# Stage 1 of a gated cross-attention and expert layer: ScalarE makes the shift of a tile, VectorE the scales of a group, and the statistics run up to eight tiles ahead

## The chip, the cores and the metric

The kernel runs on one core of a Trainium2 chip. The metric is the device time of one execution in microseconds. A core has five engines with a queue each, which run their own instructions in order and wait for each other by semaphores: TensorE (PE in the profile, PEld its weight loads), VectorE (DVE), ScalarE (ACT), GpSimd (POOL) and SyncE (SP, which here only issues transfers).

## The reference

Four batches of 1024 tokens with 1024 channels, that is 4096 tokens or 32 tiles of 128, pass two gated steps. W and b are the weights of either step, g its gate.

```python
def _L0_xattn_ref(x, adj, W, b):              # x = context (256 wide), adj = layernorm(x)
    si = jnp.einsum('bnd,d->bn', x, Wi[0])
    sj = jnp.einsum('bnd,d->bn', x, Wj[0])
    xij = jax.nn.sigmoid(si[:, :, None] + sj[:, None, :] + b[0])
    return P_ASEM * xij + (1.0 - P_ASEM) * adj

def _L0_ffn_ref(x, wg, W, b):                 # each token goes to the best of 8 experts
    logits = xt @ wg
    probs = jax.nn.softmax(logits, axis=-1)
    idx = jnp.argmax(probs, axis=-1)
    ...
    return out

x = x + jnp.tanh(g_xattn[0]) * _L0_xattn_ref(ctx_512, _layernorm(x), L0_xattn_W, L0_xattn_b)
x = x + jnp.tanh(g_ffn[0]) * _L0_ffn_ref(_layernorm(x), L0_ffn_wg, L0_ffn_W, L0_ffn_b)
```

## The kernel before

**Two stages.** Stage 1 makes the first step for every token, finds each token's expert and its place in that expert's list, and writes the row to a table in DRAM, sorted by expert. Stage 2 goes through the table in slots of 128 rows, loads each expert's weights, multiplies (L1151) and scatters the results. The change touches stage 1 alone. The sigmoid is written as a half tanh, and the first step becomes, for a token, x * a + b + c * tanh(...), where a (the scale) comes from the variance of x, and b (the shift) from the mean of x times a and the mean of the tanh.

**Tiles, groups, slots.** Stage 1 runs over 32 tiles `t`; four make a group `g`, and `r` is a tile's place in it (`GR = 4`). A tile lies in `xr`, in one of 16 slots (`RX = 16`, slot `t % 16`). SP loads the first 16 tiles at once. Tile `t` from 16 on is loaded (`next_tile`, L304) after the store of tile `t - 16` has landed (`row_stored`).

**The order.** Each engine's order is written out by hand, as a loop over the tiles. For one tile:

- VectorE: `stats` (two BN statistics, L797) and `moments` (L802) of tile `t + LEAD`, with `LEAD = 6`; `add_tanh(t)` (L808) adds the tanh. For a group: `choose` (L818 to L824, picks the expert; in the loop at `r == 1` of the next group) and `position` (L830 to L837, the places in the table; at `r == 2` of the next group).
- ScalarE: `half_tanh` (L633) of tile `t + 3`, which also sums the tanh; there are four tanh buffers, so it waits for `add_tanh` four tiles before it. `copy_turned(t)` (L641), and per group `logits_copy` (L648). The context's `context_copy`, `context_sums` and `context_spread` stand between, once per group up to tile 17.
- POOL: `norm_scalars(g)` (L470 to L475) makes the row numbers, the root of the variance and the scales of a group; `linear(t)` is the shift (L480, one element per token) and x * a + b (L482, 1024 elements). POOL makes the tile two ahead, and stores (`store`, L490, an indirect transfer) tiles of the group before: at `r == 3` the first two, behind `linear(t + 2)`; the other two at the next `r == 0` and `r == 1`. A store waits for `position` of its group.
- TensorE: `turn_tile(t)` (L1075), `logits_by_token` (L1097, at `r == 1` for the group before), `rank` (at `r == 2`), `route(t - 1)` (L1087), and the context's matmuls.

Semaphores tie them: `mv_ready` counts moments, `th_ready` tanh, `lin_ready` linears, `xc_ready` finished tiles, `pos_ready` positions of groups, `x_landed` loads of a slot. VectorE's own loop before the change is

```python
for t in range(T):
    add_tanh(t)
    if r == 2 and g > 0:
        position(g - 1)
    if t + LEAD < T:
        stats(t + LEAD)
        moments(t + LEAD)
    if r == 1 and g > 0:
        choose(g - 1)
```

## Time and profile before

| | us |
|---|---|
| three runs: median (lowest to highest) | 615.59 (614.61 to 615.63) |
| the profiled execution | 615.98 |
| its span, first to last instruction | 614.3 |

| engine | busy us | share of the span | instructions |
|---|---|---|---|
| TensorE | 506.9 | 83% | 2889 |
| VectorE | 404.8 | 66% | 529 |
| POOL | 361.5 | 59% | 537 |
| ScalarE | 293.0 | 48% | 426 |

The shares are means over both stages. Stage 1 is the stretch up to about 157 us, in which TensorE is 55 to 77% busy; from 200 us on it is nearly always busy. The rows below are of five views: windows (busy time of each engine in a stretch), the chain of waits (followed back from the last instruction, at each step to what released it), timelines of one engine in order of time, groups of instructions by line, and transfers from issue to landing. Times of rows are us from the start of the span; in brackets stands how long the engine was idle ahead of the instruction, and who ended that.

### The profile page before, as it was taken

The page shows a single profiled execution, that of the slowest core. Times are in us where ns is not written, and L with a number is a line of the kernel's source. Part 1 is how long each engine was busy: PE and PEld are TensorE (multiplying, and loading weights), DVE is VectorE, ACT ScalarE, POOL GpSimd, SP SyncE. Part 2 cuts the span into 40 slices and gives each one's busy share as a digit, 9 for nine tenths or more (in the row PEclk, how much of TensorE's full clock was granted, in tenths as well). Part 3 has the DMA queues.
Part 4 walks back from the last instruction along what each step waited for, and adds up shares of the span by engine and source line. Part 5 has one row for each costly group of instructions (what it writes and reads, how often), then busy time and mean ns, then how long its engine had stood idle before and what let it go on. Part 6 is the DMA issues. An engine that isn't in the chain of part 4 may idle for free.

```text
span 614.3 us, 14917 instructions
## 1 busy us (share of the span) xinstructions
PE 506.9 (83%) x2889; PEld 416.4 (68%) x2890; DVE 404.8 (66%) x529; ACT 293.0 (48%) x426; POOL 361.5 (59%) x537
## 2 busy tenths in 40 slices
PE   4676676666404999999999999999999999989980
PEld 4565565545303887887888888788888888878860
DVE  1777557785786777777777577778657857764230
ACT  2486556754312455455544454555445534553330
POOL 2596878889611364565555645655556465556662
PEclk9598778887755999999999999999999999999995
DMA  6952776783788588787888688897759777885520
GB/s 229 359 203 95 251 246 237 220 308 131 268 275 225 165 253 218 240 261 227 244 250 238 191 224 240 241 252 238 233 150 273 219 224 200 238 235 164 192 100 8
DMA packets 87751, 134.63 MB, mean 219 GB/s; under 512 B 11696, under 2 KB 69552, under 8 KB 87728
## 3 DMA queue, kind: packets, MB, share of 16 engines
q1 hardware_dynamic: 72464, 80.28, 46.6%
q0 software_dynamic: 15264, 54.06, 24.9%
q8 instruction: 12, 0.20, 0.1%
q14 instruction: 11, 0.09, 0.0%
HBM read 100.49 MB, written 35.91 MB: 222 GB/s over the span
## 4 chain that ended last, share of the span: by engine, by line
PE 21%; issue 19%; POOL 17%; DVE 16%; ACT 12%; ACTq 7%; DMA 2%; POOLq 2%; DVEq 1%; SPq 1%
PE pair L1151 13%; DVE xt L876 5%; DVE pair L884 5%; ACT rb L699 4%; ACT xt L691 4%; POOL scal L525 3%; POOL scal L528 3%; POOL table L490 2%; PE pair L1075 2%; PE pair L1066 2%; ACTq L732 2%; DVE xr L808 2%; DMA gates<-in_L_xattn_b 1%; ACT th L633 1%; POOL out_x L569 1%
## 5 line engine op out<-in xcount | busy, mean ns | idle before, releaser
L1151 PE MATMUL pair<-wt,xt 128*128 x1728 | 398.9, 393 | 31.8 <-DVE xt L876 27.3
L1151 PEld LDWEIGHTS pair<-wt,xt 128*128 128x128 f32 x1728 | 326.1, 189 | 104.3 <-issue 33.6
L536 POOL TENSOR_TENSOR rows<-rows,rb 128x1024 f32<-128x1024 f32 x37 | 89.5, 2420 | 2.9 <-ACT rb L713 1.6
L876 DVE TENSOR_TENSOR xt<-pair,xt 128x1024 f32 (+1 forms) x38 | 46.5, 1224 | 66.0 <-ACT xt L691 66.0
L685 ACT ACTIVATE wt<-pair 128x1024 f32 x56 | 57.6, 1028 | 55.9 <-DVE pair L884 51.7
L713 ACT ACTIVATE rb<-bias_bc,scal 128x1024 f32 (+1 forms) x37 | 46.0, 1244 | 71.1 <-POOL scal L532 71.1
L891 DVE TENSOR_TENSOR wt<-pair,wt 128x1024 f32 x56 | 67.9, 1212 | 13.0 <-ACT wt L685 13.0
L884 DVE STREAM_TRANSPOSE pair<-w_raw 128x1024 f32<-128x1024 f32 x56 | 69.4, 1239 | 1.0
L1075 PE MATMUL pair<-ident,xr 128*128 128x128 f32 x256 | 43.3, 324 | 31.6 <-DVE xr L808 31.5
L1075 PEld LDWEIGHTS pair<-ident,xr 128*128 128x128 f32 x256 | 35.9, 171 | 38.1 <-DVE xr L808 32.3
L295 POOL DMA_DIRECT2D rows<-table x38 | 23.2, 610 | 57.6 <-issue 27.0
L871 DVE STREAM_TRANSPOSE pair<-xb 128x1024 f32<-128x1024 f32 x38 | 47.8, 1259 | 12.9 <-issue 6.4
L569 POOL DMA_INDIRECT out_x<-rows,scatter_row x36 | 39.6, 1100 | 27.8 <-issue 27.8
L903 DVE SCALAR_TENSOR_TENSOR rows<-pair,scal,rows 128x1024 f32 x36 | 46.2, 1284 | 8.4 <-PE pair L1151 4.2
L490 POOL DMA_INDIRECT table<-xr,pos x32 | 42.9, 1341 | 10.3 <-issue 6.8
L641 ACT ACTIVATE xc_tr<-pair 128x1024 f32<-128x1024 f32 x32 | 32.8, 1025 | 32.7 <-PE pair L1075 32.5
L691 ACT ACTIVATE xt<-pair 128x1024 f32 (+1 forms) x38 | 39.0, 1027 | 16.3 <-DVE pair L871 10.6
L699 ACT ACTIVATE rb<-rows 128x1024 f32 (+1 forms) x37 | 38.9, 1052 | 14.4 <-POOL rows L536 14.4
L808 DVE SCALAR_TENSOR_TENSOR xr<-th,c,xr 128x1024 f32<-128x1024 f32 x32 | 41.8, 1305 | 5.3 <-POOL xr L482 5.2
L482 POOL TENSOR_SCALAR xr<-xr,ln_a,ln_b 128x1024 f32<-128x1024 f32 x32 | 41.2, 1289 | 3.2
L797 DVE BATCH_NORM_STATS2 raw<-xr 128x6 f32<-128x512 f32 x64 | 40.7, 677 | 3.2 <-DMA xr<-in_x 3.2
L705 ACT ACTIVATE ez<-rows,scal 128x8 f32 (+1 forms) x37 | 11.1, 301 | 61.1 <-POOL scal L525 61.1
(138 smaller groups left out, 407.5 us busy)
## 6 DMA issues: line engine op xcount, KB each, us to landing
w_raw<-in_L_ffn_W SPq DMA_DIRECT2D x264, 128.0 KB, 3.0
xb<-table SPq DMA_DIRECT2D x156, 128.0 KB
rows<-table POOLq DMA_DIRECT2D x38, 520.0 KB, 5.0
xr<-in_x SPq DMA_DIRECT2D x32, 512.0 KB, 6.3
ctx_in<-in_ctx SPq DMA_DIRECT2D x8, 512.0 KB, 5.3
bias_bc<-in_L_ffn_b SPq DMA_DIRECT2D x8, 512.0 KB, 6.2
out_x<-rows,scatter_row POOLq DMA_INDIRECT x36, 3.7
table<-xr,pos POOLq DMA_INDIRECT x32, 5.7
```

What stands on the lines that cost most here:

```text
L490: nc.gpsimd.indirect_dma_start(out=table, out_offset=bass.IndirectOffsetOnAxis(ap=pos[:, t:t + 1], axis=0), in_=xr[:, s, :], in_offset=Non ...
L536: nc.gpsimd.tensor_tensor(rows[:, k, 0:H], rows[:, k, 0:H], rb[:, :], ALU.add).then_inc(base_ready, 1)
L685: nc.scalar.activation(wt[:, bass.ds(par, 1), 0, :, bass.ds(column + P * n, P)].rearrange("p a k o -> p (a k) o"), ps[:, :].rearrange("p ( ...
L691: nc.scalar.activation(xt[:, bass.ds(k, 1), 0, :, :].rearrange("p a k n -> p (a k n)"), ps[:, :], ACT.Copy).then_inc(xt_hi_ready, 1)
L699: nc.scalar.activation(rb[:, :], rows[:, at, 0:H].rearrange("p a h -> p (a h)"), ACT.Square, accum_out=scal[:, at, 0:1].rearrange("p a e - ...
L808: nc.vector.scalar_tensor_tensor(out=xr[:, s, 0:H], in0=th[:, t % RTH, :], scalar=c2[:, 0:1], in1=xr[:, s, 0:H], op0=ALU.mult, op1=ALU.add ...
L871: nc.vector.transpose(turned(ps), blocked(xb[:, k, :, :])).then_inc(xb_turned, 1)
L876: nc.vector.tensor_tensor(xt[:, at, 1, :, :].rearrange("p a k n -> p (a k n)"), ps[:, :], xt[:, at, 0, :, :].rearrange("p a k n -> p (a k ...
L884: nc.vector.transpose(turned(ps), blocked(w_raw[:, n, :, :])).then_inc(w_turned, 1)
L891: nc.vector.tensor_tensor(where[:, :, 1].rearrange("p a k o -> p (a k) o"), ps[:, :].rearrange("p (k o) -> p k o", k=K), where[:, :, 0].re ...
L1075: last = nc.tensor.transpose(xt_ps[t % 2][:, P * k:P * (k + 1)], xr[:, slot_of(t), P * k:P * (k + 1)], ident[:, :])
L1151: last = nc.tensor.matmul(out_ps[r % 2][:, HALF * h:HALF * (h + 1)], xt[:, r % RING, x_part, k, :], wt[:, bass.ds(par, 1), w_part, k, HALF ...
```

## The change

Of `norm_scalars`, POOL keeps the row numbers, the addition of epsilon and the root; this is now `row_numbers(g)`, called at `r == 0` in place of `r == 2`. The scales `ln_a` and their product with the mean, `ln_ma` (now with the other sign), are made by VectorE in a new `norm_scalars(g)`, after `add_tanh` at `r == 1`. The shift `ln_b` is made by ScalarE in a new `shift(t)`, one tile behind the tanh and ahead of `copy_turned`. `linear` on POOL is one instruction and waits for `scales_of_tile` and `shift_ready`. VectorE's statistics start with six tiles as before, and then at each tile up to two more are made, as long as they are at most eight ahead (`t + LEAD + 2`). Three semaphores are new.

```diff
-                link(nc.gpsimd.tensor_scalar(ln_a[:, four], ln_r[:, four], c_ln[:, 0:1], 1.0, ALU.mult, ALU.add))
-                link(nc.gpsimd.tensor_tensor(ln_ma[:, four], of_group(g, MEAN), ln_a[:, four], ALU.mult))
+                nc.gpsimd.tensor_tensor(ln_r[:, four], ln_v[:, four], minus_half[:, :],
+                                        ALU.pow).then_inc(root_ready, 1)
             def linear(t):
                 s = slot_of(t)
-                pool.wait_ge(th_ready, t + 1)
-                link(nc.gpsimd.tensor_scalar(ln_b[:, t:t + 1], xr[:, s, TH:TH + 1], nc2h[:, 0:1], ln_ma[:, t:t + 1],
-                                             ALU.mult, ALU.subtract))
+                pool.wait_ge(scales_of_tile, t // GR + 1)
+                pool.wait_ge(shift_ready, t + 1)
...
-            norm_scalars(0)
+            row_numbers(0)
             linear(0)
             linear(1)
             for t in range(T):
                 g, r = t // GR, t % GR
-                if r == 2 and g + 1 < NG:
-                    norm_scalars(g + 1)
+                if r == 0 and g + 1 < NG:
+                    row_numbers(g + 1)
...
+            def shift(t):
+                act.wait_ge(th_ready, t + 1)
+                act.wait_ge(scales_of_tile, t // GR + 1)
+                nc.scalar.activation(ln_b[:, t:t + 1], xr[:, slot_of(t), TH:TH + 1], ACT.Identity,
+                                     scale=nc2h[:, 0:1], bias=ln_ma[:, t:t + 1]).then_inc(shift_ready, 1)
...
             for t in range(RTH - 1):
                 half_tanh(t)
+                if t:
+                    shift(t - 1)
             for t in range(T):
                 g, r = t // GR, t % GR
                 if t + RTH - 1 < T:
                     half_tanh(t + RTH - 1)
                 if r == 1 and g > 0:
                     logits_copy(g - 1)
+                if t + RTH - 2 < T:
+                    shift(t + RTH - 2)
                 copy_turned(t)
...
+            def norm_scalars(g):
+                four = slice(GR * g, GR * (g + 1))
+                dve.wait_ge(root_ready, g + 1)
+                link(nc.vector.tensor_scalar(ln_a[:, four], ln_r[:, four], c_ln[:, 0:1], 1.0, ALU.mult, ALU.add))
+                nc.vector.scalar_tensor_tensor(out=ln_ma[:, four], in0=of_group(g, MEAN), scalar=-1.0,
+                                               in1=ln_a[:, four], op0=ALU.mult, op1=ALU.mult).then_inc(scales_of_tile, 1)
...
             for t in range(LEAD):
                 stats(t)
                 moments(t)
+                if t == GR:
+                    norm_scalars(0)
+            seen = LEAD
             for t in range(T):
                 g, r = t // GR, t % GR
                 add_tanh(t)
+                if r == 1 and g + 1 < NG:
+                    norm_scalars(g + 1)
                 if r == 2 and g > 0:
                     position(g - 1)
-                if t + LEAD < T:
-                    stats(t + LEAD)
-                    moments(t + LEAD)
+                for n in range(2):
+                    if seen < T and seen <= t + LEAD + 2:
+                        stats(seen)
+                        moments(seen)
+                        seen += 1
```

VectorE around tiles 8 and 9, before: add_tanh(8), the statistics of tile 14 (which wait for the load of slot 14), add_tanh(9), the statistics of tile 15, and the first row of choose(1).

```order
L808 SCALAR_TENSOR_TENSOR xr<-th,c2,xr 128x1024 [waits lin_ready]
L797 BN_STATS raw<-xr 128x6 [waits x_landed14]
L797 BN_STATS raw<-xr 128x6
L802 BN_AGGR xr<-raw 128x2 [waits raw_ready]
L808 SCALAR_TENSOR_TENSOR xr<-th,c2,xr 128x1024 [waits lin_ready]
L797 BN_STATS raw<-xr 128x6 [waits x_landed15]
L797 BN_STATS raw<-xr 128x6
L802 BN_AGGR xr<-raw 128x2 [waits raw_ready]
L818 TENSOR_REDUCE top<-pair3 128x4 [waits by_token]
```

The same place now, from add_tanh(8) to choose(1); L826 is add_tanh, L808 the statistics, L819 and L820 the scales of group 3, L836 begins choose.

```order
L826 SCALAR_TENSOR_TENSOR xr<-th,c2,xr 128x1024 [waits lin_ready]
L808 BN_STATS raw<-xr 128x6 [waits x_landed0]
L808 BN_STATS raw<-xr 128x6
L813 BN_AGGR xr<-raw 128x2 [waits raw_ready]
L826 SCALAR_TENSOR_TENSOR xr<-th,c2,xr 128x1024 [waits lin_ready]
L819 TENSOR_SCALAR ln_a<-ln_r,c_ln 128x4 [waits root_ready]
L820 SCALAR_TENSOR_TENSOR ln_ma<-xr,ln_a 128x4 [waits dve_step]
L808 BN_STATS raw<-xr 128x6 [waits x_landed1]
L808 BN_STATS raw<-xr 128x6
L813 BN_AGGR xr<-raw 128x2 [waits raw_ready]
L836 TENSOR_REDUCE top<-pair3 128x4 [waits by_token]
```

The statistics behind add_tanh(8) are now those of tile 16, the second tile of slot 0, and behind add_tanh(9) those of tile 17, the second of slot 1.

ScalarE around tiles 6 and 7, before: half_tanh(9), copy_turned(6), half_tanh(10), copy_turned(7), half_tanh(11).

```order
L633 ACTIVATE th,xr<-sj,si_half 128x1024 [waits mv_ready,xc_ready,si_ready,sj_ready]
L641 ACTIVATE xc_tr<-pair0 128x1024 [waits routed,xc_turned]
L633 ACTIVATE th,xr<-sj,si_half 128x1024 [waits mv_ready,xc_ready,si_ready,sj_ready]
L641 ACTIVATE xc_tr<-pair1 128x1024 [waits routed,xc_turned]
L633 ACTIVATE th,xr<-sj,si_half 128x1024 [waits mv_ready,xc_ready,si_ready,sj_ready]
```

The same place now; L640 is the shift, here of tiles 8 and 9, and L647 is copy_turned.

```order
L633 ACTIVATE th,xr<-sj,si_half 128x1024 [waits mv_ready,xc_ready,si_ready,sj_ready]
L640 ACTIVATE ln_b<-xr,ln_ma,nc2h 128x1 [waits scales_of_tile,th_ready]
L647 ACTIVATE xc_tr<-pair0 128x1024 [waits routed,xc_turned]
L633 ACTIVATE th,xr<-sj,si_half 128x1024 [waits mv_ready,xc_ready,si_ready,sj_ready]
L640 ACTIVATE ln_b<-xr,ln_ma,nc2h 128x1 [waits scales_of_tile,th_ready]
L647 ACTIVATE xc_tr<-pair1 128x1024 [waits routed,xc_turned]
```

What `linear(9)` on POOL waits for now, shift(9), stands behind copy_turned(6) and half_tanh(10); before it waited for half_tanh(9), ahead of both.

## Rows read from the trace of the kernel before

**Rows 1.** Windows: busy us (instructions) of PE, PEld, DVE, ACT, POOL; granted clock; DMA.

```profile
140.00:160.00 20.00, 14.74 (x172) 11.68 (x173) 10.76 (x19) 8.89 (x11) 17.80 (x16) 0.75 0.28 113
...
300.00:614.00 314.00, 293.54 (x1281) 240.24 (x1279) 198.16 (x188) 142.75 (x206) 175.87 (x278) 0.98 0.71 207
```

**Rows 2.** Chain of waits, 110 to 157 us, shares by line.

```profile
by line: POOL table L490 32.2%; issue 28.9%; POOL ln_b L480 11.8%; POOL xr L482 11.6%; POOL ln_r L473 4.6%; POOL ln_v L472 3.4%; DVE xr L808 2.8%; ACT th L633 2.7%; POOL ln_a L474 1.2%; POOLq L489 1.1%; POOL ln_ma L475 0.9%; POOL xr L470 0.
```

**Rows 3.** Timeline of VectorE: start us, us, line, operation, [idle before].

```profile
53.41 0.19 DVE L837 TENSOR_REDUCE pos<-place 128x4 uint32<-128x32 f32 x1
...
58.84 1.28 DVE L797 BATCH_NORM_STATS2 raw<-xr 128x6 f32<-128x512 f32 x2
...
60.27 1.23 DVE L808 SCALAR_TENSOR_TENSOR xr<-th,c,xr 128x1024 f32<-128x1024 f32 x1
...
67.68 0.19 DVE L818 TENSOR_REDUCE top<-pair 128x4 f32<-128x32 f32 x1 [4.73 <-PE pair L1097]
...
73.05 0.19 DVE L837 TENSOR_REDUCE pos<-place 128x4 uint32<-128x32 f32 x1
```

**Rows 4.** Timeline of POOL: the stores of tiles 0 and 12.

```profile
55.45 2.01 POOL L490 DMA_INDIRECT table<-xr,pos  x1 [0.19 <-issue]
...
112.71 1.10 POOL L490 DMA_INDIRECT table<-xr,pos  x1 [0.17 <-issue]
```

**Rows 5.** Timeline of SP: the loads of tiles 16 and 28 are issued.

```profile
59.87 0.34 SPq L304 DMA_DIRECT2D xr<-in_x  x1
...
116.22 0.33 SPq L304 DMA_DIRECT2D xr<-in_x  x1
```

**Rows 6.** DMA: the same two loads alone, size and us from issue to landing.

```profile
xr<-in_x SPq DMA_DIRECT2D x1, 512.0 KB, 4.2
...
xr<-in_x SPq DMA_DIRECT2D x1, 512.0 KB, 3.6
```

**Rows 7.** Timeline of TensorE: logits by token (L1097), turns of a tile (L1075).

```profile
66.58 1.06 PE L1097 MATMUL pair<-fold,bias_bc 128*128 128x8 f32 x8 [1.43 <-ACT bias_bc L648]
...
71.59 1.07 PE L1075 MATMUL pair<-ident,xr 128*128 128x128 f32 x8
...
84.44 1.32 PE L1097 MATMUL pair<-fold,bias_bc 128*128 128x8 f32 x8 [1.70 <-ACT bias_bc L648]
...
90.27 1.86 PE L1075 MATMUL pair<-ident,xr 128*128 128x128 f32 x8
...
103.88 1.06 PE L1097 MATMUL pair<-fold,bias_bc 128*128 128x8 f32 x8 [1.85 <-ACT bias_bc L648]
```

**Rows 8.** Timeline of VectorE, later: ends of position, add_tanh(21) and add_tanh(31).

```profile
92.51 0.19 DVE L837 TENSOR_REDUCE pos<-place 128x4 uint32<-128x32 f32 x1
...
111.16 0.19 DVE L837 TENSOR_REDUCE pos<-place 128x4 uint32<-128x32 f32 x1
...
117.92 1.23 DVE L808 SCALAR_TENSOR_TENSOR xr<-th,c,xr 128x1024 f32<-128x1024 f32 x1
...
156.20 1.28 DVE L808 SCALAR_TENSOR_TENSOR xr<-th,c,xr 128x1024 f32<-128x1024 f32 x1
```

**Rows 9.** Timeline of ScalarE: copy_turned(10) and half_tanh(14).

```profile
73.45 1.02 ACT L641 ACTIVATE xc_tr<-pair 128x1024 f32<-128x1024 f32 x1
74.35 1.15 ACT L633 ACTIVATE th<-sj,si_half 128x1024 f32<-128x1024 f32 x1
```

**Rows 10.** Groups by line, 40:170; two of the page: busy us, mean ns | idle.

```profile
L480 POOL TENSOR_SCALAR ln_b<-xr,nc2h,ln_ma 128x1 f32<-128x1 f32 x26 | 12.7, 488 | 10.2 <-ACT th L633 9.0
...
L474 POOL TENSOR_SCALAR ln_a<-ln_r,c_ln 128x4 f32<-128x4 f32 x6 | 3.6, 594 | 0.6
...
L475 POOL TENSOR_TENSOR ln_ma<-xr,ln_a 128x4 f32<-128x4 f32 x6 | 2.2, 372 | 0.5
...
L705 ACT ACTIVATE ez<-rows,scal 128x8 f32 (+1 forms) x37 | 11.1, 301 | 61.1 <-POOL scal L525 61.1
...
L797 DVE BATCH_NORM_STATS2 raw<-xr 128x6 f32<-128x512 f32 x64 | 40.7, 677 | 3.2 <-DMA xr<-in_x 3.2
```

More of the change, by code:

```diff
@@ L214, in build @@
         lin_ready = sem("lin_ready")
+        root_ready = sem("root_ready")
+        scales_of_tile = sem("scales_of_tile")
+        shift_ready = sem("shift_ready")
         xc_ready = sem("xc_ready")
@@ L270, in slot_of, with of_group @@
             return t % RX
+        def of_group(g, col):
+            s = slot_of(GR * g)
+            return xr[:, s:s + GR, col:col + 1].rearrange("p r a -> p (r a)")
         def tile_of(rows_of, t):
@@ L460, in _, with row_numbers @@
             nc.gpsimd.tensor_copy(cum[:, 0, :], cum0_f[:, :]).then_inc(cum_ready, 1)
-            pool.wait_ge(scales_ready, 1)
-            def of_group(g, col):
-                s = slot_of(GR * g)
-                return xr[:, s:s + GR, col:col + 1].rearrange("p r a -> p (r a)")
-            def norm_scalars(g):
+            def row_numbers(g):
                 four = slice(GR * g, GR * (g + 1))
@@ L655, in _ @@
                 context_spread(g)
+            act.wait_ge(scales_ready, 1)
             for t in range(RTH - 1):
                 half_tanh(t)
+                if t:
+                    shift(t - 1)
             for t in range(T):
```

1 line of the change is left out of this document (removed).

## Prediction

> **What bounds the kernel now.** I read the windows first, then the chain of waits, then VectorE's, POOL's, TensorE's and ScalarE's timelines of stage 1, and last how long single transfers took to land. The profiled execution took 615.98 us, its span is 614.3; the median of the three runs is 615.59, 0.39 below it. The change touches stage 1 alone, which ends when VectorE has finished add_tanh(31), 1.28 us after 156.20 [rows 8]. From 300 us on TensorE is busy 293.5 of 314 us [rows 1]; that stage starts later or earlier with the end of stage 1 and is otherwise as before, so I forecast how far add_tanh(31) moves and carry this to the end one to one.
>
> Stage 1 has two halves. Between 110 and 157 us the chain of waits runs nearly all through POOL: the stores L490 32%, "issue" (between POOL's own instructions) 29%, the shift L480 12%, the linear L482 12% [rows 2], and POOL is busy 17.8 of 20 us there [rows 1]. This is what the change relieves. Before that no engine is full; the work goes round VectorE, TensorE, ScalarE and POOL once per group of four tiles. add_tanh(9) starts at 60.27 [rows 3], add_tanh(21) at 117.92 [rows 8]: three groups in 57.65 us, 19.2 us each.
>
> **Where tile 16 comes from.** There are 16 tile slots. Tile 16 is loaded when tile 0 has been stored, and tile 0 is stored when position(0) has told where. position(0) ends at 53.60 (53.41 + 0.19) [rows 3]; store(0) starts at 55.45 [rows 4]; its landing lets SP issue the load at 59.87 [rows 5], which takes 4.2 us [rows 6], so tile 16 is there at 64.07. VectorE asks for it right behind position(1), at 73.24 (73.05 + 0.19) [rows 3], two tiles after the place that this change gives to the same statistics: 9 us of slack. In the changed order (shown with the change) stats(16) stands right behind add_tanh(8), where stats(14) started at 58.84 [rows 3]. That is 5.2 us before tile 16 lands. **VectorE would stand there, and behind it in its queue stand add_tanh(9), the scales, choose(1), add_tanh(10) and position(1)**, and so the next store, and so the load of tile 20. The same place comes back at tiles 12, 16 and 20, which ask for tiles 20, 24 and 28. A loop closes that was open: position, store, load, stats, position. From position(0) to stats(16) VectorE has only two statistics (1.43 each, 58.84 to 60.27) and two add_tanh (1.23) [rows 3], 5.3 us, against a store and a load that took 8.6 us the first time (55.45 to 59.87, and 4.2) and 7.1 the last (112.71 to 116.22, and 3.6) [rows 4 to 6], with 7.8 and 7.9 between. No ordering inside 5.3 us hides 7.1.
>
> The Trainium skill (DMA: Bandwidth & Descriptors, Anatomy of one DMA) gives for a transfer of POOL's kind about 2.0 us plus bytes over 436 GB/s. For half a megabyte that makes 3.2 us, and I estimate from this page 6.4 us for a store and a load together; the rows say 7.1 to 8.6. With the page's price the four waits would each be some 1.5 us shorter, which would take about 6 us off the sum below; the measurement decides.
>
> **The change part by part.**
>
> *Start, up to add_tanh(9): later by 8.8 us.* Three things. (1) Two more tiles' statistics come before add_tanh(2), 2 x 1.43 [rows 3], and each shift on ScalarE is one small instruction; the nearest row with a scale from memory is ez, 0.30 us [rows 10], and nine of them stand ahead of linear(9), 2.7 us. The two delays lie side by side and some of either falls into idle time: I take 2 us, bounds 0 and 3. (2) linear(9) used to wait for half_tanh(9). Now it waits for shift(9), which stands behind copy_turned(6) and half_tanh(10): 74.35 - 73.45 = 0.9 for the copy, 1.15 for the tanh [rows 9], 0.3 for the shift: 2.3 us. Store(0) stands behind linear(9) on POOL. Bounds 0 (position(0) is later still) and 2.8. (3) Tile 16 is then there at 55.45 + 2 + 2.3 + 7.9 (the mean of the four) = 67.6, its statistics take 1.43, and add_tanh(9) starts at 69.1 instead of 60.27. Least: 55.45 + 7.1 + 1.4 = 63.95, later by 3.7. Most: 55.45 + 5.8 + 8.6 + 1.4 = 71.25, later by 11.0.
>
> *Three groups, add_tanh(9) to add_tanh(21): 23.6 us each for 19.2, later by 13.1 us.* From one landing to the next:
> A, landing to the start of logits_by_token: statistics 1.43, add_tanh 1.23 [rows 3], 0.1 between, and TensorE's turn of the tile, 1.07 us in one row, 1.86 in another [rows 7]: 3.8 to 4.6; I take 4.3, nearer the slower turn, since TensorE stands idle ahead of it.
> B, logits to the end of position: 66.58 to 73.24, 84.44 to 92.70 (92.51 + 0.19), 103.88 to 111.35 (111.16 + 0.19) [rows 3, 7, 8], that is 6.7, 8.3 and 7.5; I take the mean, 7.5. In it lie choose, add_tanh, and on TensorE the context of the next batch and the second turn; none of this changes.
> C, position to the next store: 1.85 before (53.60 to 55.45), 1.4 in the last of these groups (111.35 to 112.71) [rows 3, 4, 8]. The store stands behind linear(t+5), and that behind the same copy, tanh and shift as above, 2.3 us more. The four places took 1.85, 2.25, 1.5 and 1.4 before; the mean of the last three, 1.7, and 2.3 make 4.0, of which I take 3.9; bounds 1.4 (no detour) and 4.5.
> D, store to landing: 7.9; bounds 7.1 and 8.6.
> Sum 23.6, bounds 19.0 and 26.0. Three times 4.4 is 13.1; bounds -0.6 and +20.4.
> POOL and ScalarE use the stall: everything up to linear(t+3) and the other two stores of the group is done when the tile lands. That is why I charge the wait once per group and not per tile.
>
> *Tail, add_tanh(21) to add_tanh(31): shorter by 5 us.* It took 156.20 - 117.92 = 38.3 us [rows 8]. POOL loses ten shifts, 0.49 each [rows 10] and 0.1 between: 5.9 us; and of two groups the scale and its product, 0.59 + 0.37 [rows 10], 1.9 us. At most 7.8, if POOL holds the whole stretch. But after the last wait it stands idle until ScalarE has copied tile 21 and made shift(24), and row_numbers(7) waits for stats(31); so two thirds of it, 5, bounds 0 and 7.8.
>
> *At nothing:* the scales on VectorE (two instructions of 128x4 per group) stand right behind add_tanh, where VectorE next waits for a tile or for the logits; without that cover they cost under 1 us per group, and the root they wait for is made during the stall. SP's later tile loads push the first weight loads later, but they are wanted only after add_tanh(31), which moves more. The steps behind stage 1 keep their order.
>
> **Sum.** 8.8 + 13.1 - 5.0 = +16.9. 615.98 + 16.9 = 632.9 on the profile's scale, 632.5 as a median.
>
> **The rivals.**
> *POOL is what counts, and the kernel gets faster.* Place: POOL, 110 to 157 us. If tiles landed before VectorE asks, only the relief is left: -7.8 in the tail, some 608 us. For it: the chain [rows 2]. It decides where store and load together take under 5.3 us after position; no row comes near, and the slots can't be freed sooner. Chance 0.07.
> *The loop closes, but at its shortest.* Groups of 19.0 us, as now, because the waits that VectorE has today for the logits (it is idle 4.73 us ahead of 67.68 [rows 3]) are eaten by the stall. Then 8.8 - 0.6 - 5 = +3.2: 619 us. For it: part of what VectorE waits for today is indeed done during the stall; against it: TensorE's context work in B lies behind the logits, not ahead of them. Chance 0.15. With the least start as well (3.7) and the whole tail relief it would be about -4.7, 611; I leave 0.02 for that and 0.04 for a sum within 0.2%.
> *The loop at its longest.* TensorE's granted clock is 0.75 of full speed on the mean in 140 to 160 us [rows 1], so it changes between its two levels (1.2 and 2.4 GHz). If it stays at the lower because TensorE idles more, every turn takes 1.86 for 1.07 [rows 7], and B is 8.3: 26.0 us a group, 8.8 + 20.4 - 5 = +24, 640 us. Chance 0.12.
> *The change does not do what it says.* From tile 16 on the statistics can't run eight ahead, since the slots hold 16 tiles of which the last eight are not stored yet. That is the forecast itself, not a rival.
>
> **How the numbers follow.** The forecast has 0.60, the longest loop 0.12, the shortest 0.15, sums within 0.2% (1.2 us, about what a measurement of this kernel can tell from no change) 0.04, faster 0.09. The range runs from the shortest loop, 619, to 643, a little over the longest; 0.13 of the chances lie below it and some hundredths above. Faster 0.09, same 0.04, slower 0.87.
>
> **What would show it.** Right: VectorE's BN statistics show idle time put down to the loading of xr, at four places, each after the add_tanh of tiles 8, 12, 16 and 20, some 5 to 7 us each and about 20 to 30 in all (before: 3.2 in the whole run [rows 10]); add_tanh(9) near 69, add_tanh(21) near 140, add_tanh(31) near 173; add_tanh(9), (13), (17), (21) 22 to 25 us apart; stage 2 as long as before. POOL's chain between 110 and 157 is gone. Wrong: statistics that never wait, or waits that only replace those for the logits, so that add_tanh(21) stands near 120; then the start and the groups were charged for time that was idle already. If the groups are 19 but the start is 9 later, step B or C was counted twice.

## The result, and the profile after

The changed kernel took 645.35 us (median of 3 runs, 643.31 to 645.74) for 615.59: 1.0464 times as long, interval 1.0427 to 1.0501. That is 29.8 us slower where 16.9 was forecast; the direction was right, and the time lies above the range (619 to 643). The profiled execution has a span of 643.7 us for 614.3, 29.4 more.

In the changed code the statistics are L808 and L813, the scales L819 and L820, add_tanh L826, choose L836 to L842, position L848 to L855 (VectorE); the root L475, the linear L482, the store L490 (POOL); the shift L640 (ScalarE); the turn of a tile L1100 and the logits by token L1122 (TensorE).

First VectorE's waits in 20 to 190 us (what was waited for: us in total, times, longest us), which answer to the last line of [rows 10], 3.2 us in the whole run before:

```profile
DVE raw L808 <- DMA xr<-in_x: 24.6, 6, 5.6
DVE place L853 <- PE pair L1135: 18.4, 7, 3.9
DVE top L836 <- PE pair L1122: 14.1, 7, 3.7
```

The same in VectorE's timeline, beside [rows 3] and [rows 8] (in brackets the idle time before and what ended it): the statistics of tiles 16, 20, 24 and 28 wait for their loads; add_tanh(9) follows the first and add_tanh(21) the last of them; add_tanh(31) ends the stage. The two rows of L855 are the ends of position(0) and position(1).

```profile
60.06 0.19 DVE L855 TENSOR_REDUCE pos<-place 128x4 uint32<-128x32 f32 x1
...
70.97 1.28 DVE L808 BATCH_NORM_STATS2 raw<-xr 128x6 f32<-128x512 f32 x2 [5.55 <-DMA xr<-in_x]
...
72.42 1.23 DVE L826 SCALAR_TENSOR_TENSOR xr<-th,c,xr 128x1024 f32<-128x1024 f32 x1
...
84.03 0.19 DVE L855 TENSOR_REDUCE pos<-place 128x4 uint32<-128x32 f32 x1
...
94.90 1.29 DVE L808 BATCH_NORM_STATS2 raw<-xr 128x6 f32<-128x512 f32 x2 [5.51 <-DMA xr<-in_x]
...
118.82 1.28 DVE L808 BATCH_NORM_STATS2 raw<-xr 128x6 f32<-128x512 f32 x2 [5.50 <-DMA xr<-in_x]
...
142.55 1.28 DVE L808 BATCH_NORM_STATS2 raw<-xr 128x6 f32<-128x512 f32 x2 [5.31 <-DMA xr<-in_x]
...
143.99 1.23 DVE L826 SCALAR_TENSOR_TENSOR xr<-th,c,xr 128x1024 f32<-128x1024 f32 x1
...
184.79 1.27 DVE L826 SCALAR_TENSOR_TENSOR xr<-th,c,xr 128x1024 f32<-128x1024 f32 x1
```

The start, in the timelines of POOL and VectorE: POOL waits for VectorE's moments before it makes the root of group 1, and VectorE waits for that root before it makes the scales.

```profile
30.75 0.14 POOL L472 IOTA xr<- 128x4 int32 x1 [1.84 <-DVE xr L813]
...
33.08 0.23 DVE L819 TENSOR_SCALAR ln_a<-ln_r,c_ln 128x4 f32<-128x4 f32 x1 [1.26 <-POOL ln_r L475]
```

POOL's timeline: linear(5) and linear(8), which wait for ScalarE's shift, and the stores of tiles 0 and 4 [rows 4].

```profile
45.08 1.20 POOL L482 TENSOR_SCALAR xr<-xr,ln_a,ln_b 128x1024 f32<-128x1024 f32 x1 [5.10 <-ACT ln_b L640]
...
60.12 1.20 POOL L482 TENSOR_SCALAR xr<-xr,ln_a,ln_b 128x1024 f32<-128x1024 f32 x1 [5.14 <-ACT ln_b L640]
...
64.09 1.25 POOL L490 DMA_INDIRECT table<-xr,pos  x1 [0.20 <-issue]
...
88.03 1.01 POOL L490 DMA_INDIRECT table<-xr,pos  x1 [0.16 <-issue]
```

POOL's linears in the page's groups (busy us, mean ns | idle before):

```profile
L482 POOL TENSOR_SCALAR xr<-xr,ln_a,ln_b 128x1024 f32<-128x1024 f32 x32 | 44.5, 1390 | 70.4 <-ACT ln_b L640 70.3
```

The chain of waits from 144 to 186 us, the tail, where before it ran through POOL [rows 2]:

```profile
by line: PE pair L1100 37.7%; DVE xr L826 22.8%; PE pair L1122 9.1%; PE pair L1112 6.2%; DVE raw L808 5.7%; DVE pick L838 5.6%; issue 2.1%; DVE xr L813 1.5%; DVE top L836 1.4%; DVE place L853 1.4%; DVE pick L837 1.4%; DVE top_pick L840 1.4%
```

POOL is gone from it, as foreseen, but the tail did not get shorter. Taken from the starts of add_tanh(9), (21) and (31), the 29.4 us are:

| | before, us | after, us | more | forecast |
|---|---|---|---|---|
| start: to add_tanh(9) | 60.27 | 72.42 | +12.15 | +8.8 |
| three groups: to add_tanh(21) | 57.65 | 71.57 | +13.9 | +13.1 |
| tail: to add_tanh(31) | 38.28 | 40.80 | +2.5 | -5.0 |
| from add_tanh(31) to the end | 458.1 | 459.0 | +0.9 | 0 |

The groups came as forecast; the tail is off by 7.5 us and the start by 3.4.

### The profile page after: what moved, and what is told of

Same layout as the page of the kernel before. It is cut to its first block, busy times and chain, and to the rows that moved or that the text cites. A ratio compares the mean times of both kernels' runs of the same rounds, so it can differ in the third digit from the quotient of the medians.

```text
span 643.7 us, 14973 instructions
## 1 busy us (share of the span) xinstructions
PE 532.7 (83%) x2889; PEld 437.1 (68%) x2890; DVE 411.8 (64%) x545; ACT 302.1 (47%) x458; POOL 330.1 (51%) x489
## 4 chain that ended last, share of the span: by engine, by line
PE 24%; issue 17%; DVE 17%; POOL 11%; ACT 11%; DMA 8%; ACTq 6%; SPq 2%; POOLq 2%; DVEq 1%
PE pair L1176 15%; PE pair L1100 4%; DVE xt L901 4%; DVE pair L909 4%; ACT rb L710 3%; DMA xr<-in_x 3%; ACT xt L702 3%; POOL scal L525 3%; POOL scal L528 2%; DVE xr L826 2%; DMA table<-xr,pos 2%; DVE raw L808 2%; DMA out_x<-rows,scatter_row 2%; ACT th L633 2%; PE pair L1091 1%
## 5 line engine op out<-in xcount | busy, mean ns | idle before, releaser
L1100 PE MATMUL pair<-ident,xr 128*128 128x128 f32 x256 | 56.7, 395 | 43.9 <-DVE xr L826 43.9
L696 ACT ACTIVATE wt<-pair 128x1024 f32 x56 | 57.6, 1028 | 55.9 <-DVE pair L909 51.9
L1100 PEld LDWEIGHTS pair<-ident,xr 128*128 128x128 f32 x256 | 46.2, 209 | 52.7 <-DVE xr L826 45.4
L482 POOL TENSOR_SCALAR xr<-xr,ln_a,ln_b 128x1024 f32<-128x1024 f32 x32 | 44.5, 1390 | 70.4 <-ACT ln_b L640 70.3
L808 DVE BATCH_NORM_STATS2 raw<-xr 128x6 f32<-128x512 f32 x64 | 40.7, 677 | 25.2 <-DMA xr<-in_x 25.2
L647 ACT ACTIVATE xc_tr<-pair 128x1024 f32<-128x1024 f32 x32 | 32.7, 1021 | 49.3 <-PE pair L1100 49.3
L710 ACT ACTIVATE rb<-rows 128x1024 f32 (+1 forms) x37 | 38.9, 1052 | 14.1 <-POOL rows L536 14.1
L490 POOL DMA_INDIRECT table<-xr,pos x32 | 34.7, 1083 | 16.8 <-DVE pos L855 10.1
L826 DVE SCALAR_TENSOR_TENSOR xr<-th,c,xr 128x1024 f32<-128x1024 f32 x32 | 40.2, 1260 | 3.7 <-POOL xr L482 3.7
```

The lines of the kernel that those rows point to most:

```text
L696: nc.scalar.activation(wt[:, bass.ds(par, 1), 0, :, bass.ds(column + P * n, P)].rearrange("p a k o -> p (a k) o"), ps[:, :].rearrange("p ( ...
L710: nc.scalar.activation(rb[:, :], rows[:, at, 0:H].rearrange("p a h -> p (a h)"), ACT.Square, accum_out=scal[:, at, 0:1].rearrange("p a e - ...
L808: last = nc.vector.bn_stats(raw[:, t % 2, h, :], xr[:, s, HALF * h:HALF * (h + 1)])
L826: nc.vector.scalar_tensor_tensor(out=xr[:, s, 0:H], in0=th[:, t % RTH, :], scalar=c2[:, 0:1], in1=xr[:, s, 0:H], op0=ALU.mult, op1=ALU.add ...
L1100: last = nc.tensor.transpose(xt_ps[t % 2][:, P * k:P * (k + 1)], xr[:, slot_of(t), P * k:P * (k + 1)], ident[:, :])
```

## Experiments

Times are medians; each ratio is to the kernel before on the same chip, with its 95% interval. The parts of stage 1 are read from add_tanh's starts as above, position(0) from its end. The "stretch" of VectorE in the tail is worked out from the trace: for each of its instructions there, the duration above that of an undisturbed one of the same kind, summed. half_tanh(0), which no edit reaches, starts between 20.3 and 22.5 us in these kernels (22.3 before, 22.5 after), so a microsecond or two between two starts can be scatter. From there on the edits count: from half_tanh(0) to linear(0) it is 1.92 us before the change and 2.84 after it, because shift(0) now stands behind half_tanh(1). Each part is read from one trace of its kernel.

| kernel | median, us | ratio | add_tanh(9) | three groups | tail | stretch |
|---|---|---|---|---|---|---|
| before | 615.59 | 1 | 60.3 | 57.6 | 38.3 | 1.9 |
| after | 645.35 | 1.0464 | 72.4 | 71.6 | 40.8 | 4.4 |
| e1 six ahead | 624.01 | 1.0118 [1.0056, 1.0180] | 68.0 | 56.7 | 41.0 | 4.0 |
| e2 eight ahead alone | 628.12 | 1.0192 [1.0131, 1.0253] | 64.1 | 65.6 | 39.4 | 2.7 |
| e3 shift at once | 637.46 | 1.0352 [1.0283, 1.0421] | 69.4 | 65.4 | 41.4 | 4.1 |
| e4 twenty slots | 624.91 | 1.0145 [1.0087, 1.0202] | 65.4 | 56.2 | 41.9 | 6.9 |
| f1 after, extra turns | 648.93 | 1.0553 [1.0526, 1.0581] | 71.3 | 74.2 | 40.4 | 4.7 |
| f2 before, extra turns | 613.24 | 0.9949 [0.9923, 0.9975] | 62.8 | 50.7 | 38.8 | 2.6 |
| f3 twenty slots, at once | 624.29 | 1.0149 [1.0123, 1.0175] | 63.9 | 55.9 | 42.7 | 7.2 |
| f4 f3 with extra turns | 621.01 | 1.0097 [1.0072, 1.0123] | 63.8 | 51.5 | 42.6 | 8.3 |
| g1 twenty slots, neither move | 616.72 | 1.0026 [0.9997, 1.0055] | 61.3 | 56.4 | 38.3 | 1.9 |
| g2 g1 with the scales on VectorE | 618.10 | 1.0042 [1.0025, 1.0060] | 63.8 | 56.2 | 38.4 | 2.5 |
| h2 g1 with the shift on ScalarE | 624.67 | 1.0144 [1.0102, 1.0186] | 62.1 | 57.8 | 45.0 | 8.0 |
| g4 linear on ScalarE | 641.56 | 1.0416 [1.0366, 1.0465] | 75.5 | 61.6 | 45.6 | 0.4 |
| h1 f3, small instruction back | 620.07 | 1.0085 [1.0057, 1.0114] | 62.8 | 57.0 | 38.7 | 2.3 |
| i1 after, small instruction back | 646.70 | 1.0491 [1.0433, 1.0548] | 73.3 | 76.3 | 39.5 | 1.1 |
| h3 before, extra turns from tile 9 | 611.90 | 0.9924 [0.9898, 0.9950] | 60.1 | 52.0 | 37.1 | 1.9 |

### The loop: e1, e2 and e4

**e1** is the changed kernel with the statistics six ahead again; the shift and the scales stay on the engines where the change puts them, the scales of a group stand behind choose, where its statistics are there, and POOL makes the root one tile later, behind the linear.

```diff
-                if r == 0 and g + 1 < NG:
-                    row_numbers(g + 1)
...
+                if r == 1 and g + 1 < NG:
+                    row_numbers(g + 1)
...
-                for n in range(2):
-                    if seen < T and seen <= t + LEAD + 2:
-                        stats(seen)
...
+                if t + LEAD < T:
+                    stats(t + LEAD)
+                    moments(t + LEAD)
                 if r == 1 and g > 0:
                     choose(g - 1)
+                if r == 1 and g + 1 < NG:
+                    norm_scalars(g + 1)
```

> The change without its run-ahead: statistics six tiles ahead as before, shift on ScalarE and scales on VectorE as in the change. Theory L (the loop store, load, statistics, position sets the time): VectorE no longer waits for loads, the groups from add_tanh(9) to add_tanh(21) go back from 23.9 to 19 to 20 us, and what is left is the shift's place on ScalarE: 614 to 624 us. Rival S (the shift stands too late on ScalarE, and the waits for loads only sit where VectorE would wait for linear anyway): groups stay near 23 us, 638 us or more. Rival C (TensorE's lower clock is the cause, whatever the wait): 630 to 640.

**e2** is the kernel before with only the run-ahead of the change (the lines that e1 takes out, put into it).

> The kernel before with the statistics up to eight tiles ahead and nothing else; POOL keeps shift and scales. L: the loop closes as in the change, but the store no longer waits for a copy, a tanh and the shift (2.3 us), so groups of 21 to 22 us, four waits for loads of about 4 us: 626 to 634 us. S: 613 to 618 us, as the kernel before.

**e4** is the changed kernel with more room: tile 16 no longer waits for tile 0 to be stored.

```diff
-    RX = 16
+    RX = 20
```

(th, ctx_in and xc_tr move into memory that is used only after stage 1, and the counts of stores per slot follow.)

> The change with 20 tile slots in place of 16 (tanh, context and turned tiles lie where the even weights lie later, to make the room). Tile 20 takes the slot of tile 0, and VectorE asks for it four tiles later than it asks for tile 16 in the change. L: no waits for loads, groups 19 to 20 us, 614 to 624 us as in the run with six ahead. S: waits move to linear, 635 us or more. C: between, with the clock of TensorE still at 0.6 in stage 1.

e1 and e4 take the loop apart at two different places, and both take 20 to 21 us off; e1 came to the upper end of what was expected, e4 to 0.9 us above it. The groups are back at 56 to 57 us, and the statistics wait for loads no longer than before. The group of e4, and below it that of e2, from their pages:

```profile
L808 DVE BATCH_NORM_STATS2 raw<-xr 128x6 f32<-128x512 f32 x64 | 40.7, 677 | 3.4 <-DMA xr<-in_x 3.4
...
L797 DVE BATCH_NORM_STATS2 raw<-xr 128x6 f32<-128x512 f32 x64 | 40.7, 677 | 24.3 <-DMA xr<-in_x 24.3
```

e2, which has the run-ahead and nothing else, waits 24.3 us for loads and loses 8 us in the groups. So the loop is shown, from both sides. What e1 and e4 leave, 8 to 9 us, is neither run-ahead nor slots: it is in the start and the tail. (The start of e1 has a price of its own: VectorE waits 3.95 us there for the root that comes later, so that its 68.0 can't be laid beside the others.)

### The place of the shift: e3 and f3

**e3** puts the shift right behind its own tanh on ScalarE instead of one tile later.

```diff
-                if t:
-                    shift(t - 1)
+                shift(t)
...
-                if t + RTH - 2 < T:
-                    shift(t + RTH - 2)
+                if t + RTH - 1 < T:
+                    shift(t + RTH - 1)
                 copy_turned(t)
```

> The change with each shift right behind its own tanh on ScalarE, one place earlier. L: four waits for loads remain, each group 2 us shorter (the store comes earlier), and the start and the tail lose a copy and a tanh ahead of linear: 626 to 636 us. S: the waits go with the detour, 612 to 620 us.

**f3** is e3 with the 20 slots of e4.

> 20 slots and the shift right behind its own tanh together: neither the loop over the loads nor the detour is left, POOL is relieved. If these two hold all that the change loses: 605 to 614 us, the tail 31 to 35. K: the tail stays near 40, now on TensorE and VectorE: 614 to 622 us.

With 16 slots the late place costs 3 us of the start and 2 us in each group: the store stands behind the linear, the linear behind the shift, and all of it is inside the loop. With 20 slots it costs 1.5 us of the start, and the median does not move (624.91 and 624.29). In neither is the tail better: 41.4 and 42.7. Both miss what was expected: e3 by 1.5 us, and f3 lies above either of its two cases, in the tail too.

### TensorE's clock: f1, f2 and f4

The granted clock in 80 to 140 us is lower after than before; the columns are busy us (instructions) of PE, PEld, DVE, ACT and POOL, then the granted clock and DMA. After:

```profile
80.00:100.00 20.00, 14.09 (x107) 11.78 (x106) 10.47 (x19) 11.09 (x20) 11.09 (x11) 0.59 0.47 161
100.00:120.00 20.00, 15.15 (x133) 12.27 (x132) 9.35 (x22) 11.10 (x20) 8.32 (x9) 0.58 0.54 175
```

To see what that costs, TensorE turns the identity eight more times ahead of each tile from tile 2 on, in the time in which it would wait for add_tanh. **f1** is the changed kernel, **f2** the kernel before and **f4** f3 with this edit:

```diff
-                pe.wait_ge(xc_ready, t + 1)
                 if t >= 2:
                     pe.wait_ge(xc_copied, t - 1)
+                    for n in range(8):
+                        nc.tensor.transpose(xt_ps[t % 2][:, P * (n % K):P * (n % K + 1)], ident[:, :], ident[:, :])
+                pe.wait_ge(xc_ready, t + 1)
```

> The change, with eight more turns of the identity on TensorE ahead of each turn of a tile, while it waits for add_tanh; the real turn overwrites them. They cost 1.1 us a tile at the higher clock, 2.0 at the lower, mostly in idle time. Theory K (what the relief of POOL uncovers is the loop of choose, add_tanh, turn, rank, position, and that loop is long because TensorE runs at the lower clock): turns fall from 1.97 to near 1.1 us, groups from 23.9 to 21.5 to 22.5, the tail from 40.8 to 36 to 38: 631 to 638 us. Rival (the tail is long because linear waits for a shift that stands behind copy_turned): 643 to 649 us, the tail stays at 40 to 41 or grows by the added turns.

> The kernel before with the same eight added turns. K: its tail is POOL's, so that stays at 38; the groups lose up to 1 us each: 608 to 615 us. If the added turns delay TensorE where it doesn't wait: 616 to 622.

> The same with the eight added turns. K: tail 35 to 37, groups 17 to 18.5 us, 603 to 612 us, faster than the kernel before. Rival: as the run without them, or some us longer.

The groups of the turns of a tile in 20 to 190 us, before, after and in f1 (busy us, mean ns | idle before), and f1's wait for loads:

```profile
L1075 PE MATMUL pair<-ident,xr 128*128 128x128 f32 x256 | 43.3, 324 | 31.6 <-DVE xr L808 31.5
...
L1100 PE MATMUL pair<-ident,xr 128*128 128x128 f32 x256 | 56.7, 395 | 43.9 <-DVE xr L826 43.9
...
L1102 PE MATMUL pair<-ident,xr 128*128 128x128 f32 x256 | 40.1, 308 | 41.6 <-DVE xr L826 41.5
...
DVE raw L808 <- DMA xr<-in_x: 29.6, 8, 6.7
```

In f1 the turns of a tile fall from 395 to 308 ns a matmul, and yet the groups take 74.2 us and VectorE still waits 29.6 us for loads. It is not the clock that closes the loop. How much of the loop's length the clock makes f1 can't tell, since its own extra turns lie in the loop. Theory K, that the low clock is what the relief of POOL uncovers, expected 631 to 638 us of f1 and 603 to 612 of f4; they took 648.93 and 621.01. Where the loop is out of the way, the clock counts in the groups, and by more than expected: f4's fall from f3's 55.9 to 51.5 us, and f2's fall from 57.6 to 50.7 us, at a granted clock of 1.00, the 2.4 GHz level all the time, for 0.79 in the same 40 us before. f2:

```profile
80.00:100.00 20.00, 16.75 (x203) 14.62 (x199) 14.40 (x30) 13.56 (x20) 17.19 (x21) 1.00 0.75 248
100.00:120.00 20.00, 16.22 (x203) 13.73 (x204) 14.60 (x35) 12.85 (x22) 17.31 (x21) 1.00 0.71 249
```

The tail gains nothing by it: in f2 it is POOL's (the chain there runs through L490 and ln_b), in f1 and f4 the extra turns stand on the chain themselves, with 13.9% and 8.3% of it, since tiles follow each other closely there.

### The two moves apart: g1, g2, h2 (and g3)

All have 20 slots and the statistics eight ahead, so that the loop is out of the way. **g1** has neither move, **g2** only the scales on VectorE, **h2** only the shift on ScalarE, at once; f3 has both. In g2 and h2 POOL makes the root as early as in the change (`r == 0`), and in h2 it has one more instruction of 128x4 per group, which negates the scales' product.

> The kernel before with 20 tile slots and the statistics eight ahead; shift and scales stay on POOL. It is the ground on which the two moves are told apart. Loop theory (all that eight ahead costs is the wait for a slot): no wait for xr above 3.5 us, groups 18.7 to 19.2 us each, tail 38 to 39, 615 to 617 us. Rival (the two more statistics ahead of add_tanh(2) cost their 2.9 us of start whatever the slots): add_tanh(9) at 63 or later, 618 to 620 us.

> 20 slots, eight ahead, the scales of a group on VectorE as in the change, the shift on POOL as before. The changed kernel with 20 slots and the shift at once took 624.3 us. If the scales are what costs the start (VectorE waits for POOL's root ahead of stats and choose, and POOL's linear waits for VectorE): add_tanh(9) at 63 to 64, position(0) ending near 57, 620 to 623 us. If the shift on ScalarE is what costs: as with neither move, 616 us, add_tanh(9) at 61.

> g3_shift_alone with the linear as before (multiply, add), since there the linear that multiplies and subtracts took 3.78 us on POOL for 1.20 and hid everything else; POOL negates the scales in one more 128x4 instruction per group. With neither move it took 616.7 us with a tail of 38.3, with the scales alone 618.1 and 38.4. If the shift makes the tail longer, by bursts of linears against VectorE: tail 41 to 43, 620 to 624 us. If it takes both moves together: tail 38 to 39, 616 to 618 us; there POOL's scales still part its linears.

The first form of h2, **g3**, kept the sign of the scales and let the linear subtract:

```diff
-                                        ALU.mult, ALU.add).then_inc(lin_ready, 1)
+                                        ALU.mult, ALU.subtract).then_inc(lin_ready, 1)
```

> 20 slots, eight ahead, the shift on ScalarE right behind its tanh, the scales on POOL as before (its linear subtracts). If the shift is what costs, through ScalarE's queue or because POOL's linears then run in bursts against VectorE: tail 41 to 43 us, 620 to 623 us, and VectorE's instructions beside POOL's are stretched by 4 us or more in the tail (1.9 before). If the scales are what costs: tail 37 to 38, 614 to 616 us.

It took 673.55 us (1.0943, 1.0883 to 1.1003) and says nothing on the shift, since the linear that subtracts takes three times as long on POOL (g3's timeline of POOL; 1.20 us elsewhere):

```profile
105.10 3.79 POOL L484 TENSOR_SCALAR xr<-xr,ln_a,ln_b 128x1024 f32<-128x1024 f32 x1
109.06 2.12 POOL L492 DMA_INDIRECT table<-xr,pos  x1 [0.18 <-issue]
111.24 3.78 POOL L484 TENSOR_SCALAR xr<-xr,ln_a,ln_b 128x1024 f32<-128x1024 f32 x1
```

The other three give an answer. With slots enough, eight ahead alone is within the noise of before (1.0026). The scales, with the earlier root, cost 2.5 us of the start; in all, the noise can't tell g2 from g1 (1.0042 and 1.0026, intervals overlap). The shift costs 1.2%, most of it in the tail: 45.0 us for 38.3, more than the 41 to 43 expected. Of g2 I had thought it possible that the scales were the culprit, at 620 to 623 us; the start came as that case says, the median did not.

g2 shows one thing more. POOL's instructions that start in its tail take 30.1 us for 33.7 in g1's, and the tail is the same, 38.4 for 38.3. The chain of waits of g2 in 120 to 160 us says why:

```profile
by line: PE pair L1092 31.9%; DVE xr L818 19.5%; PE pair L1104 9.2%; PE pair L1114 7.8%; ACT th L636 5.3%; issue 4.7%; DVE pick L830 3.4%; DVE raw L800 3.0%; DVE onehot L834 2.6%; ACT bias_bc L651 2.5%; DVE pick L829 1.5%; DVE top L828 1.5%
```

No POOL: TensorE's turns, add_tanh and choose make a second path that is just as long as POOL's was. In g2 it also carries the scales, so that how long it was in the kernel before is not measured; it can't have been over 38.3 us. POOL's relief, with the scales handed to VectorE, was worth nothing here.

### Why the tail grows: g4, h1 and i1

As long as the linear is on POOL, VectorE's stretch in the tail mostly goes with its length: 1.9 to 2.5 us where the tail is 38.3 to 38.4, 6.9 to 8.3 where it is 42 to 45. In f3's tail the onehot of choose, 0.18 us elsewhere, takes 2.67 us, and ends where two linears end that POOL ran without a break. VectorE's timeline:

```profile
143.46 0.19 DVE L840 TENSOR_TENSOR xr<-pair,top 128x32 f32<-128x32 f32 x1
143.57 2.67 DVE L841 TENSOR_TENSOR onehot<-pick,top_pick 128x32 bf16<-128x32 f32 x1
146.16 1.27 DVE L825 SCALAR_TENSOR_TENSOR xr<-th,c,xr 128x1024 f32<-128x1024 f32 x1
```

POOL's timeline of the same 3 us:

```profile
143.84 2.36 POOL L482 TENSOR_SCALAR xr<-xr,ln_a,ln_b 128x1024 f32<-128x1024 f32 x2
```

The stretched onehot is on f3's chain of waits, with 12.4% of 120 to 164 us:

```profile
by line: PE pair L1099 33.2%; DVE xr L825 21.2%; DVE onehot L841 12.4%; PE pair L1121 6.7%; PE pair L1111 5.9%; issue 5.4%; DVE raw L807 2.7%; ACT th L633 1.4%; DVE top L835 1.4%; DVE pick L836 1.4%; DVE place L852 1.4%; DVE pick L837 1.4%;
```

Before, a small instruction (ln_b) with a wait behind it stood between any two linears. **g4** takes the linear off POOL:

```diff
+                act.wait_ge(shift_ready, t + 1)
+                nc.scalar.activation(xr[:, s, 0:H], xr[:, s, 0:H], ACT.Identity,
+                                     scale=ln_a[:, t:t + 1], bias=ln_b[:, t:t + 1]).then_inc(lin_ready, 1)
```

> 20 slots, eight ahead, scales on VectorE, shift at once, and the linear of a tile on ScalarE too, right behind copy_turned of three tiles earlier, so that POOL keeps only the root, the row numbers and the stores. With the linear on POOL it took 624.3 us with a tail of 42.7, in which VectorE's instructions were stretched by 7.2 us. Theory of collisions (VectorE and POOL hold each other up, and a relieved POOL runs its linears back to back against add_tanh and choose): the stretch falls under 2 us in the tail, the tail to 36 to 38, 617 to 620 us. Rival (TensorE and VectorE's own steps set the tail, the stretch lies beside other waits): tail 41 to 43, 623 to 626 us. Third: ScalarE, 1.15 us more per tile, becomes the bound: groups of 20 us or more, 627 us or above.

The stretch falls to 0.4 us, but ScalarE, busy 48.6 of 60 us in 80 to 140, becomes the bound (its third case), so g4 decides nothing on the tail. **h1** does it the other way round: f3, with POOL's small instruction given back; its result is written to a spare column and not used.

```diff
+                link(nc.gpsimd.tensor_scalar(spare[:, t:t + 1], xr[:, s, TH:TH + 1], nc2h[:, 0:1], ln_ma[:, t:t + 1],
+                                             ALU.mult, ALU.add))
                 nc.gpsimd.tensor_scalar(xr[:, s, 0:H], xr[:, s, 0:H], ln_a[:, t:t + 1], ln_b[:, t:t + 1],
```

> The changed kernel with 20 slots and the shift at once (624.3 us, tail 42.7), to which POOL gets back its small 128x1 instruction ahead of each linear; its result goes to a spare column and is not used. POOL has more work, nobody has less. Theory of bursts (a relieved POOL runs linear behind linear, and VectorE's instruction that falls beside the pair waits for both: the onehot of 143.57 took 2.67 us for 0.18): the small instruction with its wait parts the linears, the tail falls to 38 to 40, 619 to 621 us. Rival (ScalarE's part of the shift sets the tail, or TensorE and VectorE alone): tail 42 to 44, 624 to 627 us.

POOL does more, nobody does less, and the kernel is faster: the tail falls from 42.7 to 38.7 us, the stretch from 7.2 to 2.3, and the ratios of h1 and f3 have intervals that do not touch. The same place in h1, VectorE's timeline:

```profile
141.19 0.18 DVE L844 TENSOR_TENSOR onehot<-pick,top_pick 128x32 bf16<-128x32 f32 x1
141.29 1.43 DVE L828 SCALAR_TENSOR_TENSOR xr<-th,c,xr 128x1024 f32<-128x1024 f32 x1
```

And POOL's:

```profile
141.99 0.94 POOL L483 TENSOR_SCALAR spare<-xr,nc2h,ln_ma 128x1 f32<-128x1 f32 x1
143.03 1.20 POOL L485 TENSOR_SCALAR xr<-xr,ln_a,ln_b 128x1024 f32<-128x1024 f32 x1
144.20 0.34 POOL L483 TENSOR_SCALAR spare<-xr,nc2h,ln_ma 128x1 f32<-128x1 f32 x1
```

Here it is POOL's small instruction that waits (0.94 for 0.34) while add_tanh runs. **i1** makes h1's edit on the changed kernel itself.

> The changed kernel itself (16 slots, shift late), with POOL's small 128x1 instruction back ahead of each linear, its result unused. If the bursts hold in the changed kernel as in the one with 20 slots (where this took the tail from 42.7 to 38.7): tail 38 to 39.5 for 40.8, start and groups as they are, 643 to 644 us. If the tail there is long because the last load's stall leaves POOL and VectorE out of step, and not for bursts: tail 40 to 42, 645 to 647 us. Either way the waits for xr stay at 24 to 26 us in all.

Its tail is 39.5 us for 40.8 and the stretch 1.1 for 4.4, but the kernel is no faster: with 16 slots the small instruction lies ahead of the store and so inside the loop. From position to store i1 takes 4.7, 6.3, 4.5 and 6.3 us for 3.8, VectorE waits 34.0 us for loads, where 24 to 26 were expected, and the groups grow by 4.7 us. Most of i1's tail has POOL on its chain again. So of the changed kernel's tail the bursts are worth about 1.3 us, by one trace of each, less than with 20 slots.

### A faster kernel: h3

**h3** is the kernel before with f2's extra turns from tile 9 on only (`range(8 if t > 8 else 0)`).

> The kernel before with eight more turns of the identity on TensorE ahead of each tile's turn from tile 9 on (from tile 2 on it took 613.24, groups of 16.9 us for 19.2, but add_tanh(9) at 62.8 for 60.3). If those of tiles 2 to 8 only delayed the start: add_tanh(9) at 60 to 61, groups of 17 us, 610 to 612 us. If the start needs them to get TensorE to its higher clock: 613 to 615 us.

611.90 us, 0.9924 (0.9898 to 0.9950): the start is back at 60.1, the groups keep most of the gain (52.0). It is faster than both kernels, if by less than 1%; TensorE does work that nobody needs, to keep its clock (1.00 in 80 to 120 us).

## Why the prediction was right and wrong

**The loop: right.** Statistics that stand 5.2 us before their tile, four waits of 5.3 to 5.6 us, nothing else in VectorE's queue able to pass: as forecast, and e1, e2 and e4 show it. The group of 23.9 us (forecast 23.6) splits from the rows above. A, landing at 70.97 to logits by token at 75.47 (TensorE's timeline, not shown): 4.5 for 4.3. B, to the end of position(1) at 84.22: 8.75 for 7.5. C, to the store at 88.03: 3.8 for 3.9. D, to the next landing at 94.90: 6.9 for 7.9. B lies above the bound that I gave it (8.3) and D below its own (7.1); that the sum fits is luck. In B lie turns of TensorE at a lower clock (395 ns a matmul for 324); that these made it longer is argued and not shown, since f1 has the higher clock and no shorter group, but also the extra turns. D came out at 6.7 to 6.9 us at all four places. Here the Trainium skill (DMA: Bandwidth & Descriptors, Anatomy of one DMA), from which I had estimated 6.4, was nearer than my mean of the rows of before. Those loads stood beside more other traffic (DMA share 0.70 to 0.89 in 80 to 140 us before, 0.47 to 0.54 after); that this is the reason is argued, no run varies it.

**The start: term (1) was mis-sized.** I gave 2 us, bounds 0 and 3, for two more tiles' statistics and for the shifts; position(0) ended at 60.25 for 53.60, 6.65 later. The other two terms held: the detour from position to store took 3.84 us for 1.85, 2.0 more for a forecast of 2.3, and D 6.9. Of the 6.65, eight ahead costs 1.1 (g1, position(0) at 54.7), the scales with the earlier root 2.5 (g2, 57.2), the shift itself 0.1 (f3, 57.4) and its late place 1.5 (e4, 58.9). The last 1.3 lie between e4 and the changed kernel, which differ in their slots alone; half_tanh(0) starts 1.1 later in the second, which is scatter. Counted from half_tanh(0), the five steps are 1.3, 3.6, -0.3, 1.6 and 0.2. By either count the scales are the largest, and them I had at nothing: they stand "where VectorE next waits for a tile or for the logits", and the root "is made during the stall". In the start there is no such stall. POOL makes the root of group 1 ahead of linear(2), waits there 1.84 us for the moments of tile 7, and VectorE waits 1.26 us for the root (the rows above); linear(2) starts at 33.04 for 29.63. The cover I named was that of the later groups, not of the start. The waits of 5.10 and 5.14 us of POOL are not the scales' doing, since the scales of groups 1 and 2 were ready at 34.2 and 49.0 (VectorE's timeline, not shown); they are waits for ScalarE, where the shift stands behind other work. A shift took 0.38 us for the 0.30 of my nearest row.

**The tail: the step "shorter by 5 us" failed, by 7.5.** It counted the instructions that POOL loses and took two thirds of them for gain, because POOL was on the chain. Two things stood against that. First, the chain of waits shows one path. In g2, with POOL relieved and gone from the chain, TensorE's and VectorE's path through choose, add_tanh and the turn was as long within 0.1 us, so that the relief was worth nothing. Second, a relieved POOL holds VectorE up: h1 shows it, 4.0 us with 20 slots. In the changed kernel it is visible in choose of group 6, in the timeline of VectorE, 1.95 us for 0.19:

```profile
178.58 1.95 DVE L838 TENSOR_TENSOR pick<-pick,iota_pick 128x32 f32<-128x32 f32 x1
```

It ends, at 180.53, with the linear in POOL's timeline, at 180.48; i1 puts the worth of all that at some 1.3 us here.

```profile
178.23 1.01 POOL L490 DMA_INDIRECT table<-xr,pos  x1 [0.17 <-issue]
179.28 1.20 POOL L482 TENSOR_SCALAR xr<-xr,ln_a,ln_b 128x1024 f32<-128x1024 f32 x1
```

What the remaining microsecond or so of the tail is was not settled; the turns at the lower clock are on its chain (37.7%), but f1, which raises the clock, puts its own turns in their way and does not decide it. That cause stays open.

**Rivals.** "POOL is what counts" (608) is refuted twice, by the loop and, with the loop gone, by g2 and h2: no kernel that relieves POOL is faster than before. "The loop at its shortest" (619) is refuted by groups of 23.9 us: the stall took 5.9 us off VectorE's waits for the logits (20.0 before, 14.1 after), but those for the ranks grew by 3.4 (15.0, 18.4). The rows of before, for those shown with the result:

```profile
DVE top L818 <- PE pair L1097: 20.0, 7, 5.0
DVE place L835 <- PE pair L1110: 15.0, 7, 3.8
```

"The loop at its longest" (640) had the total nearly right, by a group that was too long, 26.0, and a tail that was too short. The range failed above because its upper end added the longest loop to a tail that still gained 5 us: the bound of the tail, 0 to -7.8, excluded a loss without a reason. That 640 came near is luck: the lower clock came (0.59 and 0.58 in the rows above), and so did its B (8.75 for 8.3), but not its D and not its tail.

**The steps by runs.** Twenty slots take off 20.4 us (after to e4). The shift at once then takes off nothing clear of the noise (f3, 0.6 in the medians, 1.0149 for 1.0145 in the ratios), the shift itself 6.2 (f3 to g2), of which h1 gives back 4.2 by a small instruction, and the scales with the earlier root 1.4 (g2 to g1), which is within the noise, as is what g1 stands over the kernel before. These are steps of one ladder, so their sum is the whole by construction and proves nothing; and a step's worth depends on its place: with 16 slots the shift at once is worth 7.9 us (e3).

## What to carry to other kernels

Running further ahead is free only while a slot is free: follow the buffer round (use, store, load, use) and compare its time with the place in the queue that now asks for it. The chain of waits gives the longest path and not the next one; before relief of an engine is counted as gain, time the second path, and let the bound of a relief include a loss where that engine shares something with the one it feeds. A cover found in the steady groups must be looked for again in the start.

## What the runs showed of the hardware

- An instruction of VectorE with two inputs in SBUF is held up beside POOL's 128x1024 linear, and through the one behind it if POOL starts that without a break: 2.67 us for 0.18 (onehot, f3), and up to 4.15 for 1.23 (add_tanh, f4). The statistics of a tile, with one input, were not: 0.2 us in all over the 24 instructions of three groups. Nor was choose's first pick, with one input in PSUM: 0.19 us at all eight places in f3, four of them beside a linear. The Trainium skill (SBUF — State Buffer, SBUF: two separate sides) calls the pair of ports that the two engines share an exclusive lock, which the loser waits for during a whole instruction. The trace agrees, and shows more: two linears back to back held it as one, and a small dependent instruction between them gave VectorE its turn (h1). One thing differs: that section gives the pair to whoever starts first, and in the rows shown VectorE's instruction is listed ahead of the linear it waits for (143.57 and 143.84, 178.58 and 179.28). No run here shows why.
- POOL's 128x1024 multiply and subtract took 3.78 us (g3), the multiply and add that it stands for 1.20 in the other kernels.
- Eight unneeded turns per tile held TensorE's granted clock at 1.00 for 0.79 in 80 to 120 us, and took 6.9 us off three groups (f2).
